# ScalarE's loop of six heads begins one head later: two heads unrolled in front of it instead of one

## The chip, the cores and the metric

The kernel runs on one core of one Trainium2 chip. The metric is the device time of one execution in microseconds (us), lower is better; the time before is the median of three runs. The engines are named as the profile names them: PE (TensorE), ACT (ScalarE), DVE (VectorE), POOL (GpSimd) and SP (SyncE, which issues the transfers).

## What is computed

A block of a transformer on 4 sequences of 2048 tokens of width 256, in float32: layer norm, then 16-head attention (head width 16) beside a mixture of 16 small experts with routing by top-k, both added to the input. The change touches the attention alone:

```python
q = (hidden_states @ Wq.T + bq).reshape(b, s, HEADS, HEAD_DIM)   # k and v alike
q = q * SCALE
scores = jnp.einsum('bqhd,bkhd->bhqk', q, k)
probs = jax.nn.softmax(scores.astype(jnp.float32), axis=-1).astype(scores.dtype)
out = jnp.einsum('bhqk,bkhd->bqhd', probs, v).reshape(b, s, d)
```

With 4 sequences of 16 heads there are 64 attention problems of 2048 queries by 2048 keys. The kernel numbers them 0 to 63 and calls each a head.

## The kernel before, in words

Four stages follow each other: `norm` (layer norm, values, routing logits), `project` (queries and keys, routing), `attend` (L487 to L874) and `finish` (experts, output projection, second norm). `attend` takes from about 240 to 3000 us of the span.

In `attend` the engines run the same sequence of heads side by side, tied only by semaphores.

- PE (`step`, L794) goes through 16 tiles of 128 keys (ST). For each it computes the scores against all 2048 queries in five pieces (NP; `score`, L775: three of 512 columns and two of 256) into three PSUM buffers `s_ps`, the weighted sum of the values of two tiles earlier (`weigh`, L783), and, in between, four matmuls of a first pass over a later head, whose only purpose is the row maximum (`pass1`, L763).
- ACT (`step`, L738) turns each piece into `prob` by an exponential (`exp`, L720): 80 of them for a head, each waiting for its score, and the first of a tile also for `weighed`. After piece 2 of tile 12 it rounds the next head's shift (`round_shift`, L727), after piece 2 of tile 1 it copies out the sums of the head before (`collect`, L733). The three `s_ps` buffers are all that lies between PE and ACT.
- DVE reduces the first pass to row maxima (`maxima`, L844), POOL copies values, splits shifts and does a search beside it, SP issues the loads and stores of each head (`feed`, `put_shift`, `put_att`, `put_split`, `put_moved`).

Each engine has a program of its own and writes its heads as one rolled loop of six heads (U = 6, ROUNDS = 10) with some heads unrolled in front and behind: ACT, PE, POOL and SP have head 0 in front, heads 1 to 60 in the loop, 61 to 63 behind. In a rolled head the values that a wait compares with are computed by register instructions (ALU_OP), in an unrolled head they are constants. L749 to L751 are ACT's loop, L752 and L753 its heads behind. The buffers are picked by `slot(r, kt, j) % R` and `tile(r, kt) % R` with R = 3; six heads turn through them a whole number of times, so the loop may begin at any head.

Of the kernel before, what the change touches and what calls it, by code (L numbers as in the profile page):

```python
# [48 lines left out]
HEADS = B * H  # L49
# [437 lines left out]
def attend(nc, sem, sb, ps, t):  # L487
    R = 3
    U = 6
# [11 lines left out]
    ROUNDS = (HEADS - 4) // U  # L501
# [49 lines left out]
    def slot(g, kt, j):  # L551
        return g * SLOTS + kt * NP + j

    def cols(j):
        return slice(CUTS[j], CUTS[j + 1])

    def wide(j):
        return slice(0, CUTS[j + 1] - CUTS[j])

    def tile(g, kt):  # L560
        return g * ST + kt

    with nc.Block() as block:
# [148 lines left out]
        @block.scalar  # L712
        def _(act):
            act.sem_inc(exped, R)
            act.sem_inc(att_read, 1)
            act.wait_ge(ones_set, 1)
            for u in range(2):
                act.activation(k_feat[u][96:P, :], prob[0][96:P, :], ACT.Copy).then_inc(ones_made, 1)

            def exp(g, r, kt, j):  # L720
                if j == 0:
                    act.wait_ge(weighed, tile(g, kt) + 1)
                act.wait_ge(scored, slot(g, kt, j) + 1)
                act.activation(prob[tile(r, kt) % R][:, cols(j)], s_ps[slot(r, kt, j) % R][:, wide(j)],  # L724
                               ACT.Exp).then_inc(exped, 1)

            def round_shift(n, r):  # L727
                if not (isinstance(n, int) and n == 0):
                    act.wait_ge(shift_turned, n)
                act.wait_ge(row_maxed, n + 1)  # L730
                act.activation(shift[:, 0, :], row_max[r % R][:, :], ACT.Copy).then_inc(shift_rounded, 1)  # L731

            def collect(g):  # L733
                act.wait_ge(weighed, tile(g + 1, 0) + R)
                act.wait_ge(att_out, (g + 1) * 16)
                act.activation(att[:, :], a_ps[:, :], ACT.Copy).then_inc(att_read, 1)

            def step(g, r, first=False, following=True):  # L738
                for kt in range(ST):
                    for j in range(NP):  # L740
                        exp(g, r, kt, j)
                        if following and (kt, j) == (ROUND_AT, 2):
                            round_shift(g + 1, r + 1)
                        if not first and (kt, j) == (LAG - 1, 2):
                            collect(g - 1)

            round_shift(0, 0)
            step(0, 0, first=True)
            with nc.Fori(0, ROUNDS, engines=[ENGINE.Activation], hint_back_edge=True) as i:  # L749
                for r in range(1, U + 1):  # L750
                    step(i * U + r, r)  # L751
            for g in range(1 + ROUNDS * U, HEADS):  # L752
                step(g, g, following=g + 1 < HEADS)  # L753
            collect(HEADS - 1)

# [586 lines left out]
```

## Time and profile before

| what | value |
|---|---|
| median of the runs | 3489.64 us |
| the three runs | 3489.64, 3498.64, 3488.87 us |
| time of the profiled execution | 3480.91 us |
| its span (first to last instruction) | 3479.2 us |
| mean granted TensorE clock | 0.974 |

The span is the stretch that all rows below are measured in, from its first instruction; 1.7 us of the profiled execution's time lie outside it. "Idle before" in a row is the time an engine stood still before the instruction, with what released it; "issue" there means that nothing in the profile was waited for, so that the engine had no instruction to run. ACTq and DVEq are the sequencers of the engines, on which waits, register instructions and branches run. q8 and q14 among the DMA queues carry instructions, not data. A loop pass of six heads begins, on ACT, at 860.0, 1111.6, 1363.9 us and so on.

### The profile page before, as it was taken

The numbers are of one execution on the slowest core, as the hardware profiler recorded it, in microseconds if no ns is written. First come the engines' busy times: TensorE is split into PE (matmuls) and PEld (weight loads), VectorE is DVE, ScalarE is ACT, GpSimd is POOL, SyncE is SP. The second block draws the span as 40 slices with busy tenths as digits, with TensorE's granted clock in tenths as the row PEclk, the third lists the DMA queues.
The fourth block names the chain that finished last, engine by engine and source line by source line (L and its number), as shares of the span: only waits on it lengthen the run. The fifth ranks groups of instructions, "written<-read, shape, count | busy, mean of one in ns | idle before, by whom it ended". The sixth has DMA issues, their size and how long they took to land. (4 is left out here: it accounts for less than half of the span.)

```text
span 3479.2 us, 74610 instructions
## 1 busy us (share of the span) xinstructions
PE 3313.0 (95%) x20848; PEld 1662.5 (48%) x20848; DVE 2895.0 (83%) x2987; ACT 2528.7 (73%) x5726; POOL 931.4 (27%) x1339
## 2 busy tenths in 40 slices
PE   7869999999999999999999999999999999599998
PEld 6423444444444444444444444444444444288887
DVE  7508999898998999998998998998998998267777
ACT  3552888888888888887888888888887888543433
POOL 2550222222222222222222222222222222144443
PEclk9986999999999999999999999999999999899999
DMA  6680112122111111111121111221111111355553
GB/s 198 178 233 31 50 53 57 52 61 58 54 56 56 53 56 54 53 53 53 53 58 54 56 55 54 59 58 54 56 54 53 53 53 47 113 136 163 163 165 115
DMA packets 133063, 272.29 MB, mean 78 GB/s; under 512 B 22512, under 2 KB 68656, under 8 KB 120432
## 3 DMA queue, kind: packets, MB, share of 16 engines
q1 hardware_dynamic: 130464, 266.68, 26.6%
q8 instruction: 176, 2.88, 0.4%
q10 hardware_dynamic: 2256, 1.36, 0.1%
q14 instruction: 167, 1.37, 0.1%
HBM read 173.59 MB, written 84.93 MB: 74 GB/s over the span
## 5 line engine op out<-in xcount | busy, mean ns | idle before, releaser
L851 DVE TENSOR_REDUCE half_max<-m_ps 128x1 f32<-128x1024 f32 x2048 | 2414.2, 1220 | 359.9 <-PE m_ps L770 344.8
L724 ACT ACTIVATE prob<-s_ps 128x512 f32<-128x512 f32 (+1 forms) x5120 | 2190.2, 521 | 459.7 <-PE s_ps L780 439.6
L780 PE MATMUL s_ps<-q_feat,k_feat 50*128 50x512 f32 (+1 forms) x5120 | 1548.7, 399 | 28.5 <-ACT prob L724 21.1
L770 PE MATMUL m_ps<-k_feat,q_feat 48*128 48x512 f32 x4096 | 1441.5, 455 | 54.8 <-DMA k_feat<-k_parts 28.3
L780 PEld LDWEIGHTS s_ps<-q_feat,k_feat 50*128 50x128 f32 x5120 | 800.8, 185 | 1063.7 <-ACT prob L724 931.6
L789 PE MATMUL a_ps<-prob,v_head 128*32 128x512 f32 x8192 | 1099.0, 609 | 0.0
L770 PEld LDWEIGHTS m_ps<-k_feat,q_feat 48*128 48x128 f32 x4096 | 684.1, 188 | 286.1 <-DVE half_max L851 246.6
L579 POOL TENSOR_TENSOR shift<-row_max,shift 128x16 fp32r<-128x16 f32 x64 | 14.3, 223 | 1236.0 <-ACT shift L731 1236.0
L789 PEld LDWEIGHTS a_ps<-prob,v_head 128*32 128x32 f32 x8192 | 161.4, 108 | 255.4 <-issue 206.9
L1133 ACT ACTIVATE g_hi<-g 128x512 fp32r<-128x512 f32 x128 | 81.0, 632 | 243.4 <-DVE g L1171 200.5
L1296 POOL TENSOR_TENSOR g_lo<-g,g_hi 128x512 fp32r<-128x512 f32 x128 | 173.2, 1353 | 229.8 <-ACT g_hi L1133 229.8
L606 POOL TENSOR_SCALAR step_of<-route,cand 64x256 f32<-64x256 f32 x217 | 199.0, 917 | 44.5 <-POOL held L607 38.3
L573 POOL COPY v_head<-v_all 128x256 f32 (+1 forms) x64 | 25.4, 398 | 671.8 <-PE a_ps L789 671.7
L607 POOL TENSOR_TENSOR held<-held,step_of 64x256 f32<-64x256 f32 x217 | 157.8, 727 | 39.8 <-POOL step_of L606 39.8
L1171 DVE TENSOR_TENSOR g<-g,mask_bc 128x512 f32<-128x512 f32 x128 | 133.5, 1043 | 35.8 <-ACT g L1130 30.5
L1066 PE MATMUL o_ps<-w_hi,g_hi 128*128 128x256 f32 x512 | 145.6, 284 | 6.8 <-issue 4.4
L1066 PE MATMUL o_ps<-w_lo,g_hi 128*128 128x256 f32 x512 | 145.2, 284 | 0.0
L1066 PE MATMUL o_ps<-w_hi,g_lo 128*128 128x256 f32 x512 | 144.0, 281 | 0.0
L1055 PE MATMUL h_ps<-xn_hi,w_hi 128*128 128x512 f32 x256 | 105.2, 411 | 31.8 <-DMA b_rows<-b_parts 31.8
L1130 ACT ACTIVATE g<-h_ps,b_col 128x512 f32<-128x512 f32 x128 | 86.2, 674 | 26.5 <-PE h_ps L1055 26.5
L1066 PEld LDWEIGHTS o_ps<-w_hi,g_hi 128*128 128x128 f32 x512 | 97.3, 190 | 12.7 <-issue 7.8
L1055 PE MATMUL h_ps<-xn_hi,w_lo 128*128 128x512 f32 x256 | 101.1, 395 | 0.0
(132 smaller groups left out, 1905.7 us busy)
## 6 DMA issues: line engine op xcount, KB each, us to landing
q_feat<-q_parts SPq DMA_DIRECT2D x128, 256.0 KB
k_feat<-k_parts SPq DMA_DIRECT2D x128, 256.0 KB
q_parts<-parts SPq DMA_DIRECT2D x32, 512.0 KB, 4.7
k_parts<-parts SPq DMA_DIRECT2D x32, 512.0 KB, 4.8
q_feat<-q_parts SPq DMA_DIRECT2D x128, 128.0 KB
k_feat<-k_parts SPq DMA_DIRECT2D x128, 128.0 KB
att_dram<-att SPq DMA_DIRECT2D x64, 256.0 KB, 14.1
mask_bc<-mask_b SPq DMA_DIRECT2D x128, 128.0 KB, 4.5
```

The costliest lines, as they stand in the source:

```text
L606: do(pool.tensor_scalar(step_of[:, :], t["route"][:, c * PART:(c + 1) * PART], bound, None, ALU.is_ge))
L607: do(pool.tensor_tensor(held[:, :], held[:, :], step_of[:, :], ALU.add))
L724: act.activation(prob[tile(r, kt) % R][:, cols(j)], s_ps[slot(r, kt, j) % R][:, wide(j)], ACT.Exp).then_inc(exped, 1)
L770: ins = pe.matmul(m_ps[p % 2][:, k * BLK:(k + 1) * BLK], q_feat[r % 2][LOW, qt * P:(qt + 1) * P], k_feat[r % 2][LOW, key:key + BLK], start ...
L780: pe.matmul(s_ps[slot(r, kt, j) % R][:, wide(j)], k_feat[r % 2][UP, kt * P:(kt + 1) * P], q_feat[r % 2][UP, cols(j)], start=True, stop=Tru ...
L789: ins = pe.matmul(a_ps[qb * VW:(qb + 1) * VW, :], v_head[r % R][:, kt, :], prob[tile(r, kt) % R][:, qb * BLK:(qb + 1) * BLK], start=(kt == ...
L851: dve.tensor_reduce(half_max[r][:, p // 2, p % 2:p % 2 + 1], m_ps[p % 2][:, :], AX.X, ALU.max).then_inc(maxed, 1)
L1055: ins = pe.matmul(h_ps[e % 2][:, :], w, v, start=(c == 0 and k == 0), stop=(c == KC - 1 and k == 2))
L1066: ins = pe.matmul(o_ps[k], v, w[:, e, :], start=(e == 0 and m == 0), stop=False)
L1130: act.activation(g[e % 2][:, :], h_ps[e % 2][:, :], ACT.Gelu, bias=b1_col[:, e:e + 1]).then_inc(gelu, 1)
L1171: dve.tensor_tensor(g[e % 2][:, :], g[e % 2][:, :], mask_bc[q % 2][:, e % QTR, :], ALU.mult).then_inc(gated, 1)
L1296: pool.tensor_tensor(g_lo[e % 2][:, :], g[e % 2][:, :], g_hi[e % 2][:, :].bitcast(F32), ALU.subtract).then_inc(split, 1)
```

## The change

Head 1 leaves the loop and is written out in front of it, with constants; the loop runs over heads 2 to 61, still ten passes of six; heads 62 and 63 are left behind it. The loops of the other four engines stay as they are.

```diff
             round_shift(0, 0)
             step(0, 0, first=True)
+            step(1, 1)
             with nc.Fori(0, ROUNDS, engines=[ENGINE.Activation], hint_back_edge=True) as i:
-                for r in range(1, U + 1):
+                for r in range(2, U + 2):
                     step(i * U + r, r)
-            for g in range(1 + ROUNDS * U, HEADS):
+            for g in range(2 + ROUNDS * U, HEADS):
                 step(g, g, following=g + 1 < HEADS)
             collect(HEADS - 1)
```

## Rows read from the trace of the kernel before

**Rows 1.** The profile's page: the span, and busy time of each engine.
```profile
span 3479.2 us, 74610 instructions
PE 3313.0 (95%) x20848; PEld 1662.5 (48%) x20848; DVE 2895.0 (83%) x2987; ACT 2528.7 (73%) x5726; POOL 931.4 (27%) x1339
```
**Rows 2.** Busy time by stretch: the nine heads behind ACT's back branch; one, and the sum.
```profile
core 0: us, PE busy (x) PEld busy (x) DVE busy (x) ACT busy (x) POOL busy (x), PEclk, DMA share, GB/s
1363.90:1407.00 43.10, 40.82 (x273) 17.54 (x272) 37.70 (x35) 34.82 (x82) 2.51 (x4) 1.00 0.17 50
sum 407.90, PE 378.73 PEld 162.67 DVE 339.24 ACT 315.23 POOL 22.65; mean PE 42.08 PEld 18.07 DVE 37.69 ACT 35.02 POOL 2.52
```
**Rows 3.** The same view: sum over the nine heads that follow those.
```profile
sum 369.90, PE 367.96 PEld 160.09 DVE 341.91 ACT 312.57 POOL 153.53; mean PE 40.88 PEld 17.79 DVE 37.99 ACT 34.73 POOL 17.06
```
**Rows 4.** The same view: sums over exponentials 26 to 80, heads of rows 2, then rows 3.
```profile
sum 260.20, PE 251.68 PEld 109.52 DVE 236.08 ACT 212.65 POOL 19.05; mean PE 27.96 PEld 12.17 DVE 26.23 ACT 23.63 POOL 2.12
sum 252.90, PE 250.96 PEld 109.27 DVE 235.42 ACT 211.96 POOL 89.07; mean PE 27.88 PEld 12.14 DVE 26.16 ACT 23.55 POOL 9.90
```
**Rows 5.** Timeline of ACT, 1110.8 to 1123 us: start, us, what, idle before.
```profile
1116.01 0.38 ACT L724 ACTIVATE prob<-s_ps 128x256 f32<-128x256 f32 x1
1119.49 1.85 ACT L724 ACTIVATE prob<-s_ps 128x256 f32<-128x256 f32 x4 [3.10 <-issue]
```
**Rows 6.** Timeline of PE, 1116 to 1124.5 us.
```profile
1119.92 0.50 PE L780 MATMUL s_ps<-q_feat,k_feat 50*128 50x512 f32 x1 [2.98 <-ACT prob L724]
1120.35 1.67 PE L789 MATMUL a_ps<-prob,v_head 128*32 128x512 f32 x8
```
**Rows 7.** Busy time by stretch, with the granted clock, behind that gap.
```profile
1120.80:1124.00 3.20, 3.20 (x17) 1.49 (x9) 0.78 (x1) 1.95 (x6) 0.00 (x0) 0.50 0.13 51
```
**Rows 8.** Instructions by line, one pass of ACT's loop, 859.82 to 1111.2 us.
```profile
L722 ACTq ALU_OP  x84: 35/35/35, 861.8 to 1108.3; - x84
L722 ACTq FUSED_REGOPS  x5: 37/37/37, 904.7 to 1069.6; - x5
L723 ACTq ALU_OP  x474: 35/35/35, 860.0 to 1110.7; - x158
L723 ACTq FUSED_REGOPS  x6: 37/37/37, 859.9 to 1069.7; - x6
L724 ACT ACTIVATE prob<-s_ps x480: 377/604/641, 860.0 to 1111.0; 128x512 f32<-128x512 f32 x96, 128x256 f32<-128x256 f32 x64
```
**Rows 9.** Instructions by line, from the hint to the gap, 1111.29 to 1119.3 us.
```profile
L723 ACTq ALU_OP  x8: 35/35/35, 1111.6 to 1115.5; - x8
L724 ACT ACTIVATE prob<-s_ps x10: 377/594/628, 1111.0 to 1116.0; 128x512 f32<-128x512 f32 x6, 128x256 f32<-128x256 f32 x4
```
**Rows 10.** Instructions by line, unrolled head 61 on ACT, 2872.3 to 2913.6 us.
```profile
L723 ACTq EVENT_SEMAPHORE  x15: 17/17/17, 2874.7 to 2910.8; - x15
L724 ACT ACTIVATE prob<-s_ps x80: 377/605/641, 2872.0 to 2913.3; 128x512 f32<-128x512 f32 x48, 128x256 f32<-128x256 f32 x32
```
**Rows 11.** DMA view of that pass, 859.8 to 1111.2 us: packets, MB, share.
```profile
q14 instruction: 15, 0.12, 0.1%
```
**Rows 12.** ACT's back branch, then the DMA view of 1117.7 to 1118.2 us.
```profile
L749 ACTq COMPARE_BRANCH  x1: 49/49/49, 1110.9 to 1110.9; - x1
q14 instruction: 1, 0.01, 3.9%
```
**Rows 13.** DVE's back branch, then GB/s in 40 slices of 892 to 895 us.
```profile
L857 DVEq COMPARE_BRANCH  x1: 79/79/79, 892.7 to 892.7; - x1
GB/s 0 0 0 0 0 0 0 0 0 218 0 0 0 0 0 0 0 0 0 0 0 0 0 0 109 0 0 0 0 0 0 0 0 0 0 0 0 0 0 0
```
**Rows 14.** GB/s in 40 slices, 985.2 to 986.6 us, where the third head of a pass ends.
```profile
GB/s 0 0 0 0 18 26 29 26 19 0 0 0 0 0 0 0 234 0 0 0 0 0 0 0 0 0 0 0 0 0 0 0 0 0 0 0 0 234 234 0
```
**Rows 15.** Instructions by line, the last before ACT's branch, 1109.1 to 1110.95 us.
```profile
L723 ACTq ALU_OP  x3: 35/35/35, 1109.1 to 1110.7; - x3
L724 ACT ACTIVATE prob<-s_ps x4: 384/610/628, 1108.7 to 1110.7; 128x512 f32<-128x512 f32 x3, 128x256 f32<-128x256 f32 x1
```

## The prediction

> **What bounds the kernel.** I read the busy times first. PE is busy for 95% of the span, DVE for 83%, ACT for 73% [rows 1], so time is won only where PE stands still or runs slowly. Next I cut the attention into heads. The change moves ACT's back branch, so I compared the nine heads that come right behind a taken back branch (7, 13, ... 55) with the nine that follow them: 407.9 us against 369.9 us, 45.3 against 41.1 us a head [rows 2, 3]. PE did less than that much more: the heads behind the branch are 38.0 us longer in sum. This is where the loop shows.
>
> Then I looked where in the head the 38.0 us lie. From exponential 26 to the end the nine heads take 260.2 us, the nine others 252.9 [rows 4]: 7.3 us. This part goes with DVE's own back branch, which stands there (at 892.7 us [rows 13], some 33 us into the head), and the change does not touch it. What remains, 38.0 - 7.3 = 30.7 us, lies in the first 25 exponentials.
>
> There the timeline of ACT shows one gap, 3.10 us before the exponential at 1119.49, with the releaser "issue": its score was ready, the instruction was not [rows 5]. PE waits through it, 2.98 us for ACT's `prob` [rows 6], since three score buffers hold little work. Behind the gap the granted clock is 0.50, the lower of the two levels, for the next 3.2 us [rows 7], and the eight value matmuls take 1.67 us [rows 6]. Gap and clock together make about 4 us of this head. The shortest of the nine, 43.1 us, kept a clock of 1.00 [rows 2].
>
> **Why ACT had no instruction.** The queue q14 carries instructions in packets of 8 KB (0.12 MB in 15 packets in one pass, ACT's and DVE's together) [rows 11]. ACT's back branch is at 1110.9 us, and one such packet is read between 1117.7 and 1118.2, just before ACT goes on [rows 12, 5]. So the gap is the wait for the block of code behind the one that the branch lands in. Where that block begins can be counted. From the hint to the gap there are 8 register instructions of L723 and 9 new exponentials (the tenth began before the hint) [rows 9], and one each of L722, L723's FUSED_REGOPS, L734, L735, L736, the hint and L749's FUSED_REGOPS: 24. The hint is the first of the pass, so a block begins at instruction 24, counted from 0.
>
> A block is taken as 128 instructions. A pass has 84 + 5 + 474 + 6 + 480 instructions of L722 to L724 [rows 8], five in each head for `round_shift` and `collect`, one extra of L729 and four of L749, 1084 in all. Blocks then begin at 24, 152, 280, 408, 536 and so on. The third head ends at instruction 542, and the packet expected at 536 is there: 234 GB/s in slice 16, that is at 985.8 us, 1.6 us before the head's end at 987.4 [rows 14]. I estimate that instruction 536 ran at 985.3, so a new block's successor is requested about 0.5 us after it is entered, when the transfers are quiet.
>
> **The change, term by term.** (a) Head 1 unrolled in front adds 80 exponentials and 16 waits for `weighed` (15 in the row, the first lies just outside) [rows 10], and two instructions each for `round_shift` and `collect`: 100. One unrolled head fewer stands behind the loop. The work is the same, and 100 of 1084 is no cost by itself: unrolled head 61 ran in step with PE. A head moves no transfer or queue order, since ACT issues none in `attend`; cost nothing, and PE's 40.9 us of work in 41.1 [rows 3] is the cover.
>
> (b) The loop body starts 100 instructions further on, so blocks begin 100 earlier in it, at 24 - 100 + 128 = 52 and every 128 from there. After the branch ACT now has 52 instructions to run before it needs the next block. In the present kernel that block arrived 8.6 us after the branch (1119.5 - 1110.9) [rows 5, 12], one of the slowest of nine. 52 instructions are 52/1084 of a pass of 251.6 us, 12 us. The gap goes, with the slow clock behind it, if the block is requested at the branch and not at its end. DVE shows that it is: its branch is at 892.7, and the only packet of that size behind it is in slice 24, at 893.8 us [rows 13], 1.1 us later, at once and not on demand of a gap. ACT's came 6.9 us after its branch; I put that down to the loads that SP issues at the start of a head, which no row here proves. Worth: -30.7 us.
>
> (c) The last block now begins at 52 + 8 x 128 = 1076, and the branch is instruction 1082. The block that the branch goes back to can be read only once that last block is entered. The last six instructions take about 1.8 us (L723's first of them at 1109.1, the branch at 1110.9) [rows 15, 12]. The request comes 0.5 us after entry in the same phase of a third head [rows 14], and from its packet to the next instruction ACT took 1.7 us (1117.8 to 1119.5) [rows 12, 5]. So the target is there 2.2 us after entry, and is wanted about 2.2 us after it (1.8, and 0.4 from the branch at 1110.9 to the hint at 1111.3, with which they begin [rows 9]). I take a stall of 0.2 us, 9 times: +1.8 us. Bounds: nothing, or 1.2 us a pass if the packet is held up by 1 us, +11 us (without the slow clock, which the shortest head was spared too [rows 2]).
>
> (d) ACT's branch leaves PE's, SP's and POOL's, which stay at the head before. No engine waits for a branch of another; nothing.
>
> Sum: -30.7 + 1.8 = -28.9 us. The profiled execution took 3480.9 us, so 3452.0 by its own clock. The median of the runs is 8.7 us above it; carried over, 3489.6 - 28.9 = 3460.7, say 3461.
>
> **A rule against this.** ACT goes on 0.4 us after its branch and stops only 24 instructions later [rows 5, 9]: the target was there, its successor was not. The Trainium skill, Runtime: NRT & Kernel Launch, section Instruction fetch mechanics, says that prefetch is purely sequential and that a taken branch to outside the window forces a fetch before execution can continue. By that alone the stall would travel with the branch and the time stay at 3490; the trace disagrees for a hinted branch. The page also gives blocks of 16 KiB or 256 instructions; the trace has packets of 8 KB. With blocks of 256 term (c) would vanish and the time be 3459.
>
> **Rivals.**
> *The target comes late.* Term (c) is bigger. For: six instructions are hardly any lead, today there are 34. Against: the quiet phase [rows 14]. Price: a gap of g on ACT costs about g + 1.0 us (3.10 became 46.0 - 41.1 - 0.8 = 4.1), so the gain of 3.4 us a pass is eaten up at g = 2.4, when the request goes out 2.9 us after entry and not 0.5. At g = 2 the total is about -4 us, 3486 (no change). If the packet is held as long as the one of today, 6.9 us [rows 12], then g = 6.4, 9 x 7.4 = 67 us against 30.7: +36, 3526, slower.
> *Fetch on demand.* The block behind the target is asked for only when ACT reaches its end. Today that end is 4.6 us after the branch (L723 at 1115.5) [rows 9], not far before the packet, which speaks for it; DVE's packet at 1.1 us speaks against. Then the gap moves to instruction 52 of head 8 and stays: 3490.
> *The count is off.* If a pass of the new body were seven instructions shorter, the branch would stand in the block before and (c) vanish: 3459, no other case in sign.
>
> **Chances.** Forecast with (c) between 0 and 11 us: 0.76. Late target, no change in sum: 0.07; slower: 0.08. On demand, no change: 0.07. A part of the gain lost but over 0.3% (10.5 us, about what a measurement of this kernel can tell from no change) left: 0.02. So faster 0.78, same 0.14, slower 0.08. The runs before spread over 9.8 us, so I let the range begin 8 us under the forecast, at 3453; above it takes in the no-change cases, up to 3490. The forecast's own range is 3453 to 3472.
>
> **What the next profile would show.** Heads 7, 13, ... near 42 us and no longer 45.3; heads 8, 14, ... at 41.1 to 41.5 with ACT's branch in front; no wait of ACT on "issue" of over 1 us in the attention; a clock of 1.00 throughout it; DVE's part of 7.3 us still there. A packet on q14 should follow 0.5 us behind the last block's entry, another before ACT has run 52 instructions. A gap right at the branch is the late target, a gap 12 us behind it is fetch on demand; either makes the forecast wrong.

## The result, and the profile after

The changed kernel takes 3447.05 us (median of four runs, 3444.45 to 3448.54) against 3494.14 us for the kernel before, measured beside it (3488.87 to 3511.31). The ratio is 0.9856 with a 95% interval of 0.9819 to 0.9893: faster, by 1.1 to 1.8%. In the repetition (the last experiment below) it was 0.9867 [0.9839, 0.9894]. Forecast were 3461 us and a range that began at 3453, so the direction and the mechanism came as forecast and the size did not: the gain is larger than any the range allowed.

In the profiled executions the difference is smaller than in the medians: 3480.91 us before, 3448.54 us after. The page after, to be held against [rows 1]:

```profile
span 3446.7 us, 74610 instructions
PE 3301.3 (96%) x20848; PEld 1661.7 (48%) x20848; DVE 2894.3 (84%) x2987; ACT 2525.6 (73%) x5726; POOL 929.1 (27%) x1339
```

The same number of instructions on every engine, a span 32.5 us shorter. The heads show where it went. Busy time by stretch, first heads 7, 13, ... 55 (those of [rows 2]), then heads 8, 14, ... 56 (those of [rows 3]); of each nine one and the sum:

```profile
core 0: us, PE busy (x) PEld busy (x) DVE busy (x) ACT busy (x) POOL busy (x), PEclk, DMA share, GB/s
1103.30:1145.30 42.00, 41.07 (x276) 17.94 (x273) 38.15 (x35) 34.85 (x82) 2.51 (x4) 1.00 0.18 54
sum 378.50, PE 370.02 PEld 161.45 DVE 343.66 ACT 313.76 POOL 22.59; mean PE 41.11 PEld 17.94 DVE 38.18 ACT 34.86 POOL 2.51
```
```profile
649.50:690.20 40.70, 40.49 (x271) 17.60 (x271) 37.56 (x35) 34.67 (x82) 17.01 (x30) 1.00 0.21 58
sum 367.00, PE 365.11 PEld 158.56 DVE 338.72 ACT 312.35 POOL 153.10; mean PE 40.57 PEld 17.62 DVE 37.64 ACT 34.71 POOL 17.01
```

407.9 + 369.9 = 777.8 us before, 378.5 + 367.0 = 745.5 after: 32.3 of the 32.5 us are in these 18 heads. The granted clock is 1.00 in all of them. The waits of ACT on "issue" in the exponentials, which held the gaps, shrank from the first line (before) to the second (after); columns are the sum, the count and the longest, in us:

```profile
ACT prob L724 <- issue: 18.8, 7, 3.3
```
```profile
ACT prob L724 <- issue: 1.4, 7, 0.2
```

The first line holds seven of the nine gaps; the other two, 1.46 and 1.34 us, the view puts down to a score. Together the nine are 21.6 us, each 24 instructions behind the hint. Behind eight of them the granted clock fell to the lower level, 30.7 us in all; in the changed kernel it does not fall between head 1 and 2968 us.

ACT's timeline over a back branch, which is now in front of head 8, stands against [rows 5]:

```profile
648.53 0.66 ACT L724 ACTIVATE prob<-s_ps 128x256 f32<-128x256 f32 x2 [0.42 <-PE s_ps L781]
649.46 3.75 ACT L724 ACTIVATE prob<-s_ps 128x512 f32<-128x512 f32 x8 [0.27 <-PE s_ps L781]
653.36 0.60 ACT L736 ACTIVATE att<-a_ps 128x512 f32<-128x512 f32 x1
653.85 2.12 ACT L724 ACTIVATE prob<-s_ps 128x256 f32<-128x256 f32 x5
656.40 2.13 ACT L724 ACTIVATE prob<-s_ps 128x256 f32<-128x256 f32 x5 [0.42 <-PE s_ps L781]
```

No gap at the branch and none 24 instructions behind it. The packet still comes late, it merely is not needed yet. By line, the branch and the hint behind it, then the DMA view of 654 to 655 us, which holds one instruction packet:

```profile
L750 ACTq COMPARE_BRANCH  x1: 63/63/63, 648.7 to 648.7; - x1
L750 ACTq BRANCH_PREFETCH_HINT  x1: 31/31/31, 649.2 to 649.2; - x1
```
```profile
q14 instruction: 1, 0.01, 1.9%
```

So it is read 5.3 to 6.3 us after the branch, while ACT goes on with exponentials.

### The profile page after: what moved, and what is told of

It reads as the page before. It is cut to its first block and busy times, and to the rows that moved or that the text cites. A ratio compares the mean times of both kernels' runs of the same rounds, so it can differ in the third digit from the quotient of the medians.

```text
span 3446.7 us, 74610 instructions
## 1 busy us (share of the span) xinstructions
PE 3301.3 (96%) x20848; PEld 1661.7 (48%) x20848; DVE 2894.3 (84%) x2987; ACT 2525.6 (73%) x5726; POOL 929.1 (27%) x1339
```

## The experiments

In all that use a filler, the filler is a number of increments of a semaphore that nobody waits for, placed on ACT in front of head 0, where it waits for the first maxima, and a second number behind the last head of the attention, so that the sum is 128 and the code of the last stage keeps its position to the block. The changed part reads:

```diff
+            for _ in range(AHEAD):
+                act.sem_inc(filler, 1)
             round_shift(0, 0)
             step(0, 0, first=True)
...
             collect(HEADS - 1)
+            for _ in range(BEHIND):
+                act.sem_inc(filler, 1)
```

**The position of the code alone.** The kernel before with 100 ahead and 28 behind.

> The kernel before with its loop at head 1, and 100 semaphore increments (28 more behind the loop) put in front of head 0 on ScalarE, where it stands idle before the first maxima. Only the position of its code changes. Theory 'code block': a block begins at instruction 52 of the pass, as after the change, so the wait on 'issue' behind the nine back branches goes and the span is within 3 us of the changed kernel's 3446.7 us. Rival 'the branches part': the gain came because ScalarE's branch no longer falls into the same head as those of TensorE, SyncE and GpSimd with that head's loads; here it still does, so nine gaps of 1.4 to 3.3 us stay and the span is 3475 to 3482 us.

Measured: span 3447.4 us, median 3450.31 (3447.43 to 3451.6), ratio to the kernel before 0.9883 [0.9849, 0.9916]. Timeline of ACT behind its branch at 603.6 us, still in front of head 7:

```profile
604.34 3.75 ACT L725 ACTIVATE prob<-s_ps 128x512 f32<-128x512 f32 x8 [0.27 <-PE s_ps L785]
608.23 0.60 ACT L737 ACTIVATE att<-a_ps 128x512 f32<-128x512 f32 x1
608.72 2.12 ACT L725 ACTIVATE prob<-s_ps 128x256 f32<-128x256 f32 x5
```

The nine heads behind the branch, to be held against the 407.9 us of [rows 2]:

```profile
sum 373.80, PE 365.29 PEld 158.39 DVE 338.93 ACT 312.67 POOL 22.62; mean PE 40.59 PEld 17.60 DVE 37.66 ACT 34.74 POOL 2.51
```

The whole gain comes without moving a head. That the branch leaves the company of PE's and SP's is worth nothing that shows: nine passes of ACT's loop take 2230.1 us here (branches at 603.6 to 2833.7), 2230.6 in the changed kernel (648.7 to 2879.3) and 2265.0 in the kernel before (606.9 to 2871.9).

One thing is new in this run. ACT stands still once behind the loop's exit, 123 instructions behind the branch that is not taken, and a packet of q14 is read at 2883.8 us, 1.7 us before ACT goes on. The clock is 0.50 from 2887 to 2900 us. The view names a value matmul as the releaser:

```profile
2885.47 2.13 ACT L725 ACTIVATE prob<-s_ps 128x512 f32<-128x512 f32 x5 [2.31 <-PE a_ps L794]
```

From the exit to the end the run takes 613.7 us, against 607.3 in the kernel before, so this gap gives back some 6 us of the gain.

**The old position with the moved loop.** The changed kernel with 28 ahead and 100 behind.

> The changed kernel with 28 semaphore increments in front of head 0 on ScalarE (100 behind the loop), so that a block begins at instruction 24 of the pass again, as before the change, while the loop still begins at head 2. Theory 'code block': ScalarE stands still on 'issue' 24 instructions behind each of nine back branches, now at the start of heads 8, 14, ...; about 1 us each at least (the packet came 4.9 to 5.7 us after the branch in the changed kernel and needs 1.6 us more, against 5 us of work), with the slow clock behind the longer ones: 10 to 30 us slower than the changed kernel, span 3457 to 3477. Rival 'the branches part': no difference from the changed kernel, 3446.7.

Measured: span 3482.8, median 3475.88 (3470.74 to 3499.89, ten runs), ratio to the kernel before 0.9965 [0.9945, 0.9985]. The gap is back at instruction 24, now in head 8, and so is the lower clock behind it:

```profile
653.74 1.86 ACT L725 ACTIVATE prob<-s_ps 128x256 f32<-128x256 f32 x4 [1.56 <-PE s_ps L786]
```
```profile
654.00:660.90 6.90, 6.72 (x28) 2.24 (x28) 2.65 (x3) 3.94 (x9) 5.62 (x7) 0.51 0.11 43
```

The view names a score as the releaser, because PE's matmul ended last; PE itself had waited 1.44 us for ACT. Against the run before this one, on the same chip, the medians differ by 26 us (3475.9 - 3450.3), against the changed kernel, whose runs were not taken beside these, by 29; both are in the upper part of the expected 10 to 30. By the profiles the distance to the changed kernel is 36 us, more than was expected.

By the medians some 13 us of the gain remain against the kernel before (3489.25 - 3475.88), although the gap is there nine times. In the profile the packet comes 5.0 to 5.6 us after the branch, against 4.8 to 7.1 before, and the gaps are 1.3 to 1.8 us against 1.3 to 3.3, so the place of the branch matters for how late the packet is. The profile itself shows no gain that remains, for the lower clock lasts longer (51 us in the attention against 31), and this profiled execution is the second slowest of the ten.

Together with the first run this settles the cause: what the change did is to move ACT's code by 100 instructions against the blocks it is read in.

**The target late.** The changed kernel with 123 ahead and 5 behind.

> The changed kernel with 123 semaphore increments in front of head 0 on ScalarE (5 behind the loop), so that the last block of a pass begins one instruction ahead of the branch (at 1081 of 1084) instead of six. This is the rival 'the target comes late' brought about on purpose. Theory: the packet of the target is asked for 0.5 us after entry and is there 2.2 us after entry, the branch needs it about 0.6 us after entry: a gap of about 1.6 us at each branch, no slow clock or a short one, 9 x 1.6 to 2.6 = 14 to 23 us slower than the changed kernel, span 3461 to 3470. Rival: a branch whose target has not come starts the fetch anew, gap of 5 us or more each with the slow clock, 50 us or more, span above 3495. Rival 'entry does not matter': 3447.

Measured: span 3519.3, median 3520.67 (3519.99 to 3521.97), ratio 1.0085 [1.0051, 1.0118]: slower than the kernel before, 73 us slower than the changed kernel. ACT's timeline at the branch, and PE's behind it:

```profile
647.53 0.77 ACT L725 ACTIVATE prob<-s_ps 128x256 f32<-128x256 f32 x2 [0.42 <-PE s_ps L786]
655.18 2.14 ACT L725 ACTIVATE prob<-s_ps 128x512 f32<-128x512 f32 x5 [6.88 <-issue]
```
```profile
655.83 0.58 PE L786 MATMUL s_ps<-q_feat,k_feat 50*128 50x256 f32 x1 [6.00 <-ACT prob L725]
```

My theory of a gap of 1.6 us was wrong and the rival right: 6.9 us at the branch, with one instruction packet found in the DMA view between 653.0 and 653.6 us, 5 us after the branch at 648.0. The nine gaps are 5.9 to 7.1 us.

**No hint.** The kernel before, only this:

```diff
-            with nc.Fori(0, ROUNDS, engines=[ENGINE.Activation], hint_back_edge=True) as i:
+            with nc.Fori(0, ROUNDS, engines=[ENGINE.Activation]) as i:
```

> The kernel before without hint_back_edge on ScalarE's loop alone. Theory: without the hint the target of the back branch is read only after the branch, so the gap moves to the branch itself and the one at instruction 24 comes on top or is merged with it: 3 to 8 us more for each of nine, span 3500 to 3550. Rival 'the hint does nothing on ScalarE': no difference, 3479. The code is one to three instructions shorter in a pass.

Measured: span 3528.6, median 3524.26 (3519.22 to 3530.45), ratio 1.0090 [1.0054, 1.0126].

```profile
614.25 1.85 ACT L724 ACTIVATE prob<-s_ps 128x512 f32<-128x512 f32 x4 [6.78 <-issue]
```

The same kind of gap at the branch as in the run before, nine times 6.6 to 8.8 us, and the gap at instruction 24 is gone. So a hint that gets through in time spares ACT about 7 us at each of nine branches, and one that does not saves nothing. Against the kernel before, with its own gap at instruction 24, the hint is worth 49 us of span in all, 5.5 a branch (3528.6 - 3479.2); against the run with the position alone 81 us, 9.0 a branch. Here the Trainium skill's rule (Runtime: NRT & Kernel Launch, section Instruction fetch mechanics), that a taken branch to outside the window stalls for a fetch, agrees with the trace, which puts 6.8 us to it. With the hint in time it does not hold.

**The same code position, the branch at another time.** The kernel before with 60 ahead and 68 behind, and ACT's pass cut at tile 11 of a head:

```diff
-            def step(g, r, first=False, following=True):
-                for kt in range(ST):
+            def step(g, r, first=False, following=True, tiles=range(ST)):
+                for kt in tiles:
...
+            step(1, 1, tiles=range(CUT))
             with nc.Fori(0, ROUNDS, engines=[ENGINE.Activation], hint_back_edge=True) as i:
                 for r in range(1, U + 1):
-                    step(i * U + r, r)
-            for g in range(1 + ROUNDS * U, HEADS):
+                    step(i * U + r, r, tiles=range(CUT, ST))
+                    step(i * U + r + 1, r + 1, tiles=range(CUT))
+            step(1 + ROUNDS * U, 1 + ROUNDS * U, tiles=range(CUT, ST))
+            for g in range(2 + ROUNDS * U, HEADS):
```

> The kernel before with ScalarE's loop cut inside a head: the pass begins at tile 11 of head 1, 7, ... (about 28 us into the head, when the head's transfers are over), and semaphore increments put the code so that a block begins 24 instructions behind the hint, as before the change. Theory 'the transfers hold the packet up': the packet behind the branch is read about 1.1 us after it, as DVE's was, and lands before 24 instructions (about 5 us) are over, so no gap on 'issue' and a span of 3445 to 3450 us. Rival 'ScalarE's packet always comes about 5 us after its branch, whatever the transfers do' (it did in the changed kernel and in the run with the grid alone): gaps of 1 to 3 us stay and the span is 3465 to 3482.

Measured: span 3448.5, median 3449.54 (3447.66 to 3450.29), ratio 0.9883 [0.9857, 0.9908]. The branch, GB/s in 40 slices of 883 to 886.5 us, and the ACT timeline behind it:

```profile
L754 ACTq COMPARE_BRANCH  x1: 49/49/49, 883.0 to 883.0; - x1
```
```profile
GB/s 0 0 0 0 0 0 0 0 0 0 0 0 94 0 187 0 0 0 0 0 0 0 0 0 0 0 0 0 0 0 94 0 0 0 0 0 0 0 0 0
```
```profile
883.71 2.85 ACT L726 ACTIVATE prob<-s_ps 128x512 f32<-128x512 f32 x6 [0.19 <-issue]
887.29 1.08 ACT L726 ACTIVATE prob<-s_ps 128x512 f32<-128x512 f32 x2 [0.74 <-PE s_ps L789]
```

The 8 KB packet is in slice 12, at 884.05, 1.0 us after the branch (a slice is 87.5 ns; 94 GB/s in it are 8 KB). The 187 in slice 14 are a packet of 16 KB on q8, the 94 in slice 31 a second one of 8 KB on q14, and no data moves in this stretch. At all nine back branches the first packet comes 1.0 to 1.1 us behind. So with a block that begins 24 instructions behind the hint there is still no gap: what makes the packet late is the time of the branch. In the kernel before, the first 8 us behind the branch at 1110.9 hold the loads and stores of a head's start, by the DMA view of 1110.8 to 1118.8 us:

```profile
q1 hardware_dynamic: 394, 1.16, 54.9%
```

That it is these transfers that hold the packet up is the reading that fits. I did not try to take away one of them by itself.

**Four instructions of lead.** The changed kernel with 126 ahead and 2 behind.

> The changed kernel with 126 semaphore increments in front of head 0 on ScalarE (2 behind the loop): the last block of a pass begins at instruction 1078, four ahead of the branch (1.2 us), between the six of the changed kernel (1.7 us, no gap) and the one of the run with the late target (7 us of gap). Theory 'the branch waits for a packet that is under way': asked for 0.5 us after entry, there at 2.2 us, so a gap of about 0.5 us and a span of 3447 to 3453. Rival 'any target not yet there is read anew': the full 7 us, span 3515 to 3522.

Measured: span 3471.1, median 3471.88 (3469.28 to 3473.23), ratio 0.9946 [0.9931, 0.9962]; neither number. At the branches the theory holds: from the branch at 650.9 to the hint at 651.8 us it takes 0.9 us in place of the 0.5 of the changed kernel, and ACT goes on after 0.77 (0.77 to 1.06 at the nine branches).

```profile
652.11 3.74 ACT L725 ACTIVATE prob<-s_ps 128x512 f32<-128x512 f32 x8 [0.77 <-PE s_ps L786]
```

Yet the span is 24 us longer than the changed kernel's. ACT's branches, first the changed kernel's, then this run's, tell where:

```profile
L750 ACTq COMPARE_BRANCH  x10: 44/49/63, 648.7 to 2879.3; - x10
```
```profile
L753 ACTq COMPARE_BRANCH  x10: 44/49/63, 650.9 to 2886.9; - x10
```

Two us lie ahead of the first branch, 5.4 us in the nine passes (2236.0 against 2230.6), 0.6 a pass, and 17 us behind the exit (584.2 against 567.4). There ACT stands 1.62 us until 2938.36, 124 instructions behind the loop's exit, with an instruction packet read between 2936.6 and 2937.2 us, and the clock falls to the lower level for the rest of the last head, whose 165 matmuls take 48 us:

```profile
q14 instruction: 1, 0.01, 3.4%
```
```profile
2941.00:2989.00 48.00, 48.00 (x165) 17.17 (x161) 0.00 (x0) 26.73 (x59) 0.00 (x0) 0.50 0.04 9
```

**Both: another code position and VectorE without its loop.** The kernel before with 40 ahead and 88 behind, and

```diff
-            with nc.Fori(0, ROUNDS, engines=[ENGINE.DVE], hint_back_edge=True) as i:
-                for k in range(U):
-                    maxima(i * U + R + k, k % R)
-            maxima(HEADS - 1, (HEADS - 1) % R)
+            for n in range(R, HEADS):
+                maxima(n, n % R)
```

> The version meant to be best: the kernel before with ScalarE's loop at head 1, 40 semaphore increments in front (88 behind), so that blocks begin at instruction 112 and, last, at 1008 of the pass, 74 instructions ahead of the branch, and with VectorE's loop over the maxima written out (heads 3 to 62, no back branch). If the 0.7 to 0.8 us that each head with VectorE's branch loses is the branch, 9 times 0.73 = 6.6 us more go than with the code's position alone: span 3439 to 3442, against 3447. If it is the row maximum that ends each head's reductions instead, nothing: 3447.

Measured: span 3441.1, median 3441.51 (3438.03 to 3443.86), ratio 0.9859 [0.9833, 0.9885]. The expected span is met, but by two errors that cancel: VectorE's part was worth more, and behind the loop's exit there is a gap as in the first run, here 54 instructions behind the branch that is not taken, with a packet of q14 read at 2848.6 us, 1.6 before ACT goes on, and the low clock after it:

```profile
2850.19 1.65 ACT L725 ACTIVATE prob<-s_ps 128x512 f32<-128x512 f32 x4 [4.21 <-issue]
```
```profile
2850.40:2862.00 11.60, 11.16 (x49) 4.75 (x49) 6.58 (x7) 7.57 (x17) 0.00 (x0) 0.50 0.01 3
```

**The change and VectorE without its loop**, the diff just shown on the changed kernel.

> The changed kernel with VectorE's loop over the maxima written out, ScalarE's as the change has it. The earlier version with both the filler and VectorE written out had one gap of 4.2 us where ScalarE leaves its loop, with the slow clock behind it, about 8 us in all; the changed kernel has none. If the two gains add: 3446.7 less 6.6 us for VectorE's branch and less up to 3 us for the heads in which its loop's bookkeeping shows, a span of 3436 to 3441.

Measured: span 3426.4, median 3428.59 (3427.57 to 3430.48), ratio to the kernel before 0.9825 [0.9788, 0.9861]. By the medians that is 18 us under the changed kernel's first runs and 15 under those on the same chip (the repetition below, whose profiled span of 3442.4 us is 16.0 above this one). What PE waits for DVE in the first pass, in the changed kernel and in this run:

```profile
PE m_ps L771 <- DVE half_max L852: 27.0, 79, 1.0
```
```profile
PE m_ps L771 <- DVE half_max L852: 3.5, 17, 0.5
```

**Both loops written out**, on ACT and on DVE:

```diff
-            with nc.Fori(0, ROUNDS, engines=[ENGINE.Activation], hint_back_edge=True) as i:
-                for r in range(1, U + 1):
-                    step(i * U + r, r)
-            for g in range(1 + ROUNDS * U, HEADS):
+            for g in range(1, HEADS):
                 step(g, g, following=g + 1 < HEADS)
```

> The kernel before with ScalarE's and VectorE's loops both written out: no back branch, no hint and no loop exit on either, code read in sequence only. Theory 'only branches and the exit cost': as good as the changed kernel with VectorE written out, or 1 to 2 us better, span 3434 to 3440. Rival 'longer code costs': more packets to read per head among the head's transfers; but an unrolled head has 100 instructions against 180, so fewer packets, and no gap.

Measured: span 3429.2, median 3429.23 (3427.11 to 3431.26), ratio 0.9823 [0.9787, 0.9860]: the same as the run before, within the spread of either. With its packets in time ACT's loop costs nothing that shows; DVE's does.

**The change once more**, unaltered.

> The changed kernel itself once more, five rounds against the kernel before on one chip, to settle the size. In the profiles the change is worth 32.5 us, in the medians 42 to 47. If the kernel before is slower in most of its executions because its nine races between packet and 24 instructions are lost by more than in the profiled one (its clock was 0.965 to 0.971 in thirteen of them, against 0.974), the difference of the medians is 38 to 45 us again and the spread of this kernel stays under 6 us; if the first comparison was a chance, the difference is 29 to 34.

Measured: median 3443.50 (3443.33 to 3444.74, six runs); the kernel before beside it 3490.71 (3477.20 to 3506.40, eleven runs). Ratio 0.9867 [0.9839, 0.9894]. The difference of the medians is 47 us again, above even the expected 38 to 45, and the spread of the changed kernel is 1.4 us against 29. The clock that the single executions of the kernel before were granted goes with their times: 0.974 in the one of 3477.2 us, 0.965 in the one of 3506.4. I estimate from these that the slower one ran 63 us longer at the lower level (0.009 x 3490 us, twice, since that level is half the clock), which is worth up to 31 us; the two differ by 29.

## Why the prediction was right and where it was wrong

*What bounds the kernel* held: the gain lies where the 38.0 us were found, and PE follows ACT's gaps.

*Term (b)*, -30.7 us for the gap and its clock: right in cause, and 1.6 us short in the profiled executions (32.3 us in the 18 heads, with everything else in them). The first two runs show that the position of the code alone brings the gain, and that moving the loop without it does not. It is not the only way: in the run that cuts the loop inside a head the block begins at instruction 24 as before, and the gap is gone too. The inference that the block is asked for at the branch and not at its end was right: the packet was read between 654 and 655 us, while instruction 52 came some 11 us behind the branch. The sentence that no row proved, that transfers hold ACT's packet up, is supported by the same run (1.0 us after the branch against 5.3 to 6.3), though no single transfer was taken away.

*Term (c)*, +1.8 us for the target: nothing. The 1.7 us of lead, the time from the last block's beginning to the branch, were just enough; with four instructions of lead ACT waits 0.4 us longer there and a pass is 0.6 us longer. As a risk I had priced it wrongly: I let the cost grow with the lateness of the packet, and put the worst at 6.4 us for a packet held up. In fact it is a step. With four instructions of lead the target is read ahead of the branch and ACT waits for it; with one instruction it is read only 4.3 to 5.5 us after the branch and ACT stands about 6 to 7 us. The slower rival was real, and five instructions away.

*Term (d)* and the 100 instructions of (a): nothing, as said.

*The step that failed is the last one, the carrying over to the median.* "The median of the runs is 8.7 us above it; carried over" treats the 8.7 us as something that both kernels have. The runs show that the changed kernel has nothing of the kind: its profiled execution and its median agree (3448.5 and 3447.1), and in the repetition it spread over 1.4 us where the kernel before spread over 29. So the 8.7 us belonged to the kernel before. The profiled execution that I started from was also a fast one: of the 37 others of that kernel on record, two were faster.

That the 8.7 us belong to the gaps is my reading of why. The nine waits are nine races between a packet and 24 instructions, and the profiled execution had lost them by less than most. For it speak the clocks in the repetition, and that a kernel whose gaps come for certain hardly spreads: with one instruction of lead and nine full gaps the runs lie within 2.0 us. It is not shown directly, since only one execution of the kernel before has a trace.

The miss of 13.7 us on the median (3460.7 forecast, 3447.05 measured) adds up: 8.7 us of the carrying over, 1.8 of term (c), 1.6 to 1.7 by which (b) fell short, and 1.5 by which the changed kernel's median lies under its profiled execution. Without the first the forecast would have been 3452, and a range that begins 8 us under it would have held the measured time. The measured gain of the medians is 47 us against the 28.9 of the sum.

Of the signs named for the next profile, heads 7, 13, ... came at 42.1 us and no wait on "issue" was over 0.2; heads 8, 14, ... came at 40.8, a little under the 41.1 to 41.5 named.

*The rivals.* Fetch on demand after the branch fell with the first profile, and so did the case in which the stall travels with the branch and the time stays at 3490. "The count is off" did not happen: the blocks were where they were counted.

## What to carry to other kernels

A gap on "issue" at a fixed number of instructions behind a loop's branch is code that has not been read: count the instructions to it and to the branch, and move the loop against the blocks, with a filler or an unrolled piece; keep several instructions of lead between the last block's beginning and the branch. Look behind the loop's exit too: three of the runs with a filler lost time there. When a kernel's executions spread, compare the profiled execution with the others before you carry its distance from the median over to another kernel; if the stall that you remove is a race, the distance can be a part of it. Such a change rests on counts: an edit ahead of the loop on that engine can undo it. The run with both loops written out had no such gap at all.

## What the runs showed that I had not expected

- A hinted branch whose target has not been asked for costs as much as one without a hint, 6.9 and 6.8 us in the gaps shown; with 1.2 us of lead it costs 0.6 us a pass.
- Where a hinted loop ends, the code behind it can come late: gaps of 4.21 us (54 instructions behind the exit), 2.31 us (123) and 1.62 us (124), each at the beginning of the next block by the count and each with a packet of q14 read 1.5 to 1.7 us before ACT goes on. Why it is late was not tested; in the changed kernel, whose next block begins at the same distance as in the run with 123, no such gap shows.
- One short gap can be dear where PE has little other work: 1.62 us of ACT in the last head, then 48 us at a clock of 0.50, 17 us in all. In the two heads before it, gaps of 2.31 and 4.21 us were followed by a clock of 0.50 for some 13 us.
- VectorE's loop cost 16 us of span on the same chip, over twice the 6.6 us that I had put to its branches. PE's short waits for its reductions fell from 27.0 to 3.5 us. Of the 16 us, 7.6 lie in heads 7, 13, ... (378.4 against 370.8 us in sum), in which DVE's branch stands. Which of its loop's instructions costs the rest was not tried.
- The fastest version by the median is the changed kernel with VectorE's loop written out, 3428.59 us; with both loops written out it is 3429.23, no different.
